# Two attention layers on one core: maxima in pairs, masks added by VectorE, and the heads of layer 0 taken in the order 0, 2, 1, 3

## What is computed

```
xn = layernorm(x)
x  = x + attention0(xn) + ffn0(xn)      # layer 0
xn = layernorm(x)
x  = x + attention1(xn) + ffn1(xn)      # layer 1
```

```
scores = einsum('bqhd,bkhd->bhqk', xq, xk) / sqrt(16)
scores = where(tril, scores, -inf)
out    = einsum('bhqk,bkhd->bqhd', softmax(scores), xv)
```

## Time and profile before

| | us |
|---|---|
| median of three runs | 1993.01 (1991.43 to 1997.32) |
| the profiled execution | 2006.2 |
| its span, first to last instruction | 2004.5 |
| TensorE busy in it | 1914.6 (96%) |
| VectorE busy | 1379.2 (69%) |
| ScalarE busy | 1088.6 (54%) |
| attention of layer 0, first score product to last | 498.66 to 1232.5 |
| attention of layer 1 | 1467.43 to 1968.8 |

### The profile page before, as it was taken

The page is one execution under the profiler, slowest core; times in us unless marked ns, Lnnn a source line. Parts: engine busy times, 40 slices in busy tenths (PEclk is TensorE's granted clock), DMA queues, the critical chain, the costliest instruction groups (busy, mean ns, idle before and its releaser), DMA issues.

```text
span 2004.5 us, 28840 instructions
## 1 busy us (share of the span) xinstructions
PE 1914.6 (96%) x10864; PEld 975.3 (49%) x10864; DVE 1379.2 (69%) x1719; ACT 1088.6 (54%) x2177; POOL 232.4 (12%) x606
## 2 busy tenths in 40 slices
PE   6999999999999999999999999999999999999998
PEld 5888887733333333333334335744543333333436
DVE  6554544425899999999996763756787777777733
ACT  4221212122787878878775774312257777677662
POOL 1000000000000000100000100000023433333330
PEclk9999999988999999999997899999999999999999
DMA  6010100043112211112212000103312212212102
GB/s 211 1 48 0 44 1 1 10 122 90 30 32 69 49 32 31 34 31 44 44 31 54 7 8 6 54 16 83 90 33 52 47 32 52 45 35 52 30 10 87
DMA packets 79211, 87.52 MB, mean 44 GB/s; under 512 B 19072, under 2 KB 52864, under 8 KB 79072
## 3 DMA queue, kind: packets, MB, share of 16 engines
q1 hardware_dynamic: 79072, 85.67, 17.2%
HBM read 55.20 MB, written 20.71 MB: 38 GB/s over the span
## 4 chain that ended last, share of the span: by engine, by line
PE 81%; ACT 7%; DVE 4%; SPq 4%; issue 2%; DMA 2%; POOL 0%; DVEq 0%; POOLq 0%; ACTq 0%; PEldq 0%
PE ps L1498 19%; PE ps L1528 11%; PE ps L1179 8%; PE ps L1180 7%; PE ps L1181 7%; PE ps L1435 7%; ACT arena L806 6%; PE ps L1524 6%; PE ps L1356 5%; PE ps L1362 4%; PE ps L1273 3%; SPq L468 2%; SPq L466 1%; DMA slots<-arena 1%; DVE arena L1043 1%
## 5 line engine op out<-in xcount | busy, mean ns | idle before, releaser
L806 ACT ACTIVATE arena<-ps 128x512 f32<-128x512 f32 (+3 forms) x1792 | 867.7, 556 | 325.5 <-PE ps L1528 171.4
L1043 DVE TENSOR_REDUCE arena<-ps 128x1 f32<-128x1024 f32 (+3 forms) x768 | 856.1, 1153 | 181.0 <-PE ps L1362 104.8
L1498 PE MATMUL ps<-arena 128*17 128x512 f32 (+3 forms) x3584 | 439.2, 562 | 1.0 <-ACT arena L806 0.6
L1362 PE MATMUL ps<-slots 48*128 48x512 f32 x1024 | 409.7, 474 | 8.8 <-DMA slots<-kparts 4.6
L1528 PE MATMUL ps<-slots 50*128 50x512 f32 x1024 | 387.9, 459 | 24.0 <-ACT arena L806 14.7
L1528 PEld LDWEIGHTS ps<-slots 50*128 50x128 f32 x1024 | 172.7, 188 | 326.7 <-ACT arena L806 269.1
L1524 PE MATMUL ps<-slots 98*128 98x512 bf16 (+3 forms) x768 | 207.7, 328 | 9.2 <-DMA slots<-arena 5.8
L1356 PE MATMUL ps<-slots 96*128 96x512 bf16 (+3 forms) x768 | 193.6, 328 | 13.8 <-DVE arena L1046 7.7
L1362 PEld LDWEIGHTS ps<-slots 48*128 48x128 f32 x1024 | 171.8, 190 | 66.7 <-DVE arena L1043 22.9
L606 POOL TENSOR_SCALAR_AFFINE_SELECT arena<-arena 128x128 f32<-128x128 f32 x512 | 145.3, 295 | 320.3 <-ACT arena L806 312.4
L667 ACT ACTIVATE xn<-ps 128x512 f32<-128x512 f32 (+1 forms) x44 | 26.3, 598 | 259.1 <-PE ps L1181 259.1
(11 more groups left out here) (127 smaller groups left out, 1855.3 us busy)
## 6 DMA issues: line engine op xcount, KB each, us to landing
slots<-qparts SPq DMA_DIRECT2D x96, 128.0 KB, 3.6
qparts<-arena SPq DMA_DIRECT2D x32, 256.0 KB
xnT<-arena SPq DMA_DIRECT2D x256, 32.0 KB
slots<-qparts SPq DMA_DIRECT2D x96, 64.0 KB, 3.3
qparts<-arena SPq DMA_DIRECT2D x48, 128.0 KB
slots<-qparts SPq DMA_DIRECT2D x32, 192.0 KB, 3.7
w_raw<-in_wgu SPq DMA_DIRECT2D x20, 256.0 KB, 3.2
acc<-in_x SPq DMA_DIRECT2D x4, 1024.0 KB, 8.0
```

Of the source, the lines that this page charges most:

```text
L806: act.activation(prob[local % P_RING][:, q0:CH], bank(local % SP_RING)[:, q0:CH], ACT.Exp, scale=SCALE).then_inc(S["p_ready"], 1)
L1043: dve.tensor_reduce(maxes[c][:, h[0] * TPC + qt:h[0] * TPC + qt + 1], src[:, 0:w], AX_X, ALU.max).then_inc(S["x_done"], 1)
L1362: last = pe.matmul(dst[:, k0:k1], q_slot[u][r:r + ROWS[0], c, h % 2, qt * P:(qt + 1) * P].bitcast(F32R), k_slot[u][r:r + ROWS[0], k0:k1].b ...
L1498: mm = pe.matmul(bank(7)[32 * h:32 * h + DH + 1, q0:CH], v_slot[n % SLOTS][:, kt, :], prob[idx % P_RING][:, q0:CH], start=(kt == 0), stop= ...
```

## The change

Five edits:

1. In layer 0 all groups take their main items in the head order 0, 2, 1, 3.
2. The first maxima of layer 0 come in pairs, behind k = 1 and k = 3, from projection 13 on, and the four pieces of a pair are sorted by key half, so that heads of both halves of the array alternate. `lower` moves behind k = 1. SyncE writes the first rows before the stores of projection 17, not 18 (`ROWS_AT`).
3. Behind the rows VectorE no longer waits for its own last operation before it raises `x_done`; TensorE waits for `m_ready` where it reuses that bank.
4. In layer 1, for the second half of queries (c = 1), the product that adds the mask is gone: VectorE adds the mask, widened to 1024 columns with zeros, and takes the maximum in one `tensor_tensor_reduce`, whose full result goes to the unused `w_q`.
5. The mask tile is widened from 128 to 1024 columns of bfloat16, which GpSimd fills at the start.

```diff
-FIRST_MAX_AT = 12
-ROWS_AT = [18, 20]
+FIRST_MAX_AT = 13
+ROWS_AT = [17, 20]
 
-    return [(kt, h, max(0, kt - TPC * qc) * P if causal else 0) for kt in range(kts) for h in range(HG)]
+    heads = range(HG) if causal else (0, 2, 1, 3)
+    return [(kt, h, max(0, kt - TPC * qc) * P if causal else 0) for kt in range(kts) for h in heads]
 
-    j = 3 * (i - FIRST_MAX_AT) + k
-    return range(j, j + 1) if i >= FIRST_MAX_AT and k < 3 and j < count else range(0)
+    j = 4 * (i - FIRST_MAX_AT) + k - 1
+    return range(j, min(j + 2, count)) if i >= FIRST_MAX_AT and k % 2 else range(0)
 
+def masked_by_vector(causal, c):
+
+    return causal and c > 0
 
-        mask_qk = sb("mask_qk", [P, P], BF16)
+        mask_qk = sb("mask_qk", [P, N], BF16)
...
-                    dve.wait_ge(S["m_ready"], n * QC + c + 1)
                     dve.sem_inc(S["x_done"], 1)
+
+                def reduce_maximum(src, n, c, qt, h, j):
+
+                    w, seg = max_width(l == 1, c, qt), segment(l == 1, c, qt)
+                    if masked_by_vector(l == 1, c):
+                        masked = w_q[:, 2 * (j % 2):2 * (j % 2) + 2, :].rearrange("p k f -> p (k f)")
+                        dve.tensor_tensor_reduce(out=masked[:, 0:w], in0=src[:, 0:w], in1=mask_qk[:, N - w:N], scale=1.0, scalar=LOWEST,
+                                                 op0=ALU.add, op1=ALU.max,
+                                                 accum_out=maxes[c][:, h[0] * TPC + qt:h[0] * TPC + qt + 1]).then_inc(S["x_done"], 1)
+                        return
...
-                            if k == 0 and i:
+                            if k == 1 and i:
                                 lower(i - 1)
...
                     if opens and j >= 2:
 
                         pe.wait_ge(S["x_done"], j if (n, c, qt) == (GROUPS - 1, 1, None) else j - 1)
+                        m, mc, mqt, _ = all_items[j - 2]
+                        if m is not None and mqt is None:
+                            pe.wait_ge(S["m_ready"], m * QC + mc + 1)
...
-                                         start=True, stop=k1 < w)
-                        if k1 == w:
-                            last = pe.matmul(dst[:, w - P:w], identb[:, :], mask_qk[:, :], start=False, stop=True)
+                                         start=True, stop=k1 < w or masked_by_vector(causal, c))
+                        if k1 == w and not masked_by_vector(causal, c):
+                            last = pe.matmul(dst[:, w - P:w], identb[:, :], mask_qk[:, N - P:N], start=False, stop=True)
...
-                    for piece in first:
-                        if piece[0] in items:
...
+                    todo = [piece for piece in first if piece[0] in items]
+                    if not causal:
+                        todo.sort(key=lambda piece: piece[5])
+                    for piece in todo:
```

More of the change, by code:

```diff
@@ L34 @@
 MASKED = -1e30
+LOWEST = -3e38
 SLOTS = 3
@@ L543, in _ @@
                                    pattern=[[-1, P]], channel_multiplier=1).then_inc(const_b, 1)
[L544 removed]
+            pool.affine_select(out=mask_qk[:, N - P:N], in_=mask_qk[:, N - P:N], compare_op=ALU.is_ge, fill=MASKED, base=0,
                                pattern=[[-1, P]], channel_multiplier=1).then_inc(const_b, 1)
@@ L771, in _ @@
                             split(NCH * NQ + t)
-                items = [main_items(l == 1, c) for c in range(QC)]
                 group_items = per_group[l]
@@ L801, in attend @@
                         for c in range(QC):
-                            for i, (kt, h, q0) in enumerate(items[c]):
+                            for i, (kt, h, q0) in enumerate(main_items(l == 1, c)):
                                 act.wait_ge(S["s_ready"], local + 1)
@@ L1286, in _ @@
                 causal = l == 1
-                items = [main_items(causal, c) for c in range(QC)]
                 group_items = per_group[l]
@@ L1336, in _ @@
                 blocks = max_blocks(l == 1)
-                items_in_all = sum(len(b) for b in blocks)
+                all_items = [item for b in blocks for item in b]
+                items_in_all = len(all_items)
                 starts = [sum(len(b) for b in blocks[:n]) for n in range(GROUPS)]
@@ L1443, in first_maxima @@
                 def first_maxima(items):
-                    for piece in first:
-                        if piece[0] in items:
-                            if piece[0] == 0 and piece[-2]:
-                                pe.wait_ge(S["slot_in"][0], 16 * 12)
-                                pe.wait_ge(*((S["b_evac"], TT) if l else (S["y_evac"], TT * len(ROUNDS) + 1)))
-                            max_piece(*piece)
+                    todo = [piece for piece in first if piece[0] in items]
+                    if not causal:
+                        todo.sort(key=lambda piece: piece[5])
+                    for piece in todo:
+                        if piece[0] == 0 and piece[-2]:
+                            pe.wait_ge(S["slot_in"][0], 16 * 12)
+                            pe.wait_ge(*((S["b_evac"], TT) if l else (S["y_evac"], TT * len(ROUNDS) + 1)))
+                        max_piece(*piece)
                 if l == 0:
@@ L1515, in attend @@
                         for c in range(QC):
-                            nkt = len(items[c]) // HG
-                            for i, (kt, h, q0) in enumerate(items[c]):
+                            items = main_items(causal, c)
+                            nkt = len(items) // HG
+                            for i, (kt, h, q0) in enumerate(items):
                                 if i == 0:
```

29 lines of the change are left out of this document (15 added, 14 removed).

## The result

The changed kernel takes 1969.4 us in the median of 15 runs (1964.66 to 1992.46); the kernel before, run beside it, takes 1996.8 (1983.86 to 2008.41, also 15). The ratio is 0.9886, 95% interval 0.9851 to 0.9921: faster by 1.1%. An execution over 1.5% above the fastest of its kernel counts as slow and is left out of every median and ratio here (none of these two kernels, two of `e4_heads_only`, three of `e6_singles13`, of which one took 4555.6 us). The profiled execution takes 1973.01 us against 2006.2, and its span is 33.2 us shorter.

A forecast was written before the change was run, and what follows sets the result against it. Layer 0's attention was taken as bound by the ring of three banks through ScalarE. Terms -17.2 - 12.6 - 3.0 = -32.8 us took 2006.2 to 1973.4, less 13.2 for the median: 1960 us, range 1938 to 1993.

The forecast's parts named there:

- the likeliest case: Whole kernel: the forecast of 1960 us holds, own range 1948 to 1970; chance 0.58.
- the last step: Whole kernel: from 1973.4 us for the profiled execution, 13.2 taken off for the median, giving 1960.
- First maxima (-17.2): Layer 0's first maxima: standstill and half clock go, pairs 3.21 us apart, first score product at 481.4 instead of 498.66.
- Masks (-12.6): Layer 1's second parts: 15 x 14 mask products of 0.06 us go, VectorE stays hidden; -12.6 us.
- Pauses (-3.0): VectorE behind the rows, both layers: 60 pauses shrink by some 0.1 us, half of 6 us taken; -3.0 us.
- Head order (0): Layer 0's quads: a fifth step lies in the wait for ScalarE, the quad stays 2.60 us; 0 us.
- the small slip: Rival, layer 0: the fifth step lengthens quads by 0.02 to 0.1 us, time 1965 to 1984; chance 0.09.
- The wide mask (0): Kernel start: filling the wide mask costs GpSimd under a microsecond more, ahead of any product; nothing.
- The clock didn't fall in the first maxima: Rival, layer 0's first maxima: the clock falls all the same, 17.6 us of gain lost, time 1977; chance 0.12.
- The weight load isn't paid: Rival, layer 0's quads: same-half products pay weight loads, 0.2 to 0.36 us a quad, time 2008 to 2046; chance 0.11.
- VectorE isn't the bound in layer 1: Rival, layer 1's second parts: half-speed fused operation makes VectorE the bound, 158 us, time 2130; chance 0.04.
- Group 13 kept its clock: Rival, layer 0's group 13: some 20 us of its 72.2 come back, time 1940; chance 0.06.

The follow-up runs named there:

- e4_heads_only: The kernel before with only the head order 0, 2, 1, 3 in layer 0: 1994.6 us, ratio 1.0013 to before.
- e6_singles13: The kernel before with first maxima from projection 13, one item behind each step, not paired; first rows from item 17: 1992.0 us, ratio 0.9983 to before.
- e5: The kernel before with only VectorE's pause behind the rows removed (TensorE waits for `m_ready` instead): 1993.2 us, ratio 0.9978 to before.
- e1: The changed kernel with head order 0, 1, 2, 3 restored in layer 0, all other edits kept: 1962.4 us, ratio 0.9848 to before.
- e7: The kernel before with paired first maxima but still from projection 12, first rows from item 16: 1988.0 us, ratio 0.9967 to before.
- e9: The changed kernel with head order 0, 1, 2, 3 in layer 0 and layer 1's second-part rows written ahead of stores: 1960.0 us, ratio 0.9818 to before.
- e10: The changed kernel with head order 0, 1, 2, 3 in layer 0, run once more in more rounds: 1964.1 us, ratio 0.9842 to before.
- e3: The kernel before with only the mask edits (mask added in VectorE, widened mask tile): 1982.5 us, ratio 0.9942 to before.
- e2: The kernel before with only the pairs of first maxima, from projection 13: 1979.3 us, ratio 0.9937 to before.
- e8: The kernel before with layer 0's maxima in head order 0, 2, 1, 3 instead of 2, 0, 3, 1: 2046.9 us, ratio 1.0238 to before.

## Why the prediction was right, and where it was off

**The time.** 1960 was forecast, 1969.4 measured, inside the range of 1938 to 1993 and at the edge of the likeliest case's own (1948 to 1970). The forecast for the profiled execution, 1973.4, met its 1973.01, but only since errors cancelled there; that is luck. The 9.4 us by which the median was missed all lie in the last step, where I took off 13.2 us because the profiled execution before stood that far above its median: the one after stood only 3.6 above. Against the sum of -32.8, the first maxima gave 3.0 more and group 13 gave 17.2 that were not in it; the masks and pauses together gave 10.3 instead of 15.6 (5.3 less), the head order cost 5.2, group 11 and the last group 5.3 (each holds a fall of the clock of 6.8 us that the trace before doesn't have there), a fall in layer 1 (one group of 32.99 us) and small things there 3.3, the ends 0.7. That is -20.2 and +19.8. The median gained 27.4, not 33.2: the trace before was of an execution 9.4 us above the median of its 15 runs, that of after 3.6 above; 33.2 - 9.4 + 3.6 = 27.4. I read the length of falls in one trace as part of the kernel: "what followed the standstill" was a fall of 24 us in that trace and in e5, and of 6.8 to 13.7 in four others, and group 13 "at clock 0.69" took 55 us at full clock in seven of the ten traces of other kernels whose quads are as long (after, e1 to e7, e9, e10). The floor that I gave for group 13 at full clock, 47 us, was too low.

**First maxima (-17.2).** Mechanism right: the standstill gone, and with it the half clock; e7 and the count over all traces show the one with the other. The pace was mis-sized: 2.95 us a pair for 3.21. I said that a pair opens "only when both reductions of the pair before are done". Its first piece needs the bank of the first of these reductions alone, and starts while the second runs (444.96). When that ends (445.37), the opening piece of the pair's other item and the closing piece of the first item start together on the two halves (445.42), and the reduction 0.54 later: 0.60 us between reductions, not 0.85. With 2.95 us a pair the last one opens at 471.4, not 474.4, and that is the 3.0. Of a fall of 13.7 us, as e3 and e4 show it, the gain is 14.9, of which 4.8 is the later start (e7 against e2) and the rest the pairs and the length of the fall, which no run separates; not all of it shows in the timed runs, where the pairs alone gave 0.6% in the ratio (some 12 us), and 10.1 us in the column "at 0.990", which leaves the clock's share out.

**Masks (-12.6).** Mechanism right, 0.06 us each where TensorE is the bound (0.11 to 0.12 a quad with two). The first two quads of the second part wait for VectorE or a DMA and give 0.04 and 0.03 instead of 0.12 each; a group gives 0.66 to 0.69, not 0.84, in all 10 us. VectorE stays hidden. The reading of the accumulator was taken as 0.10 us on top of a reduction; fused operation and reading together are 0.01 to 0.02 longer than a plain reduction, although the record of the reading says 0.08. The Trainium skill (VectorE: DVE Perf Modes, Two Vector instructions with no wait between them) has such an operation as two instructions: the trace shows both, and their price is nearly that of one.

**Pauses (-3.0).** Nothing; the price was the wrong step. The pause did go (in layer 1 the next operation starts 0.21 us behind the start of the last row operation, 1602.73 to 1602.94 in the trace after, where the earlier trace rows have 0.43; in layer 0 of e5 it is 0.34), but VectorE had idle time in the next quad to catch up, and what it hands over earlier lies ahead of the wait of the fourth score product. I had taken half without a reason; "at least none where VectorE catches up anyway" was the case.

**Head order (0).** Right for the plain quad in what counts: the fourth score product at 1.18, the closing piece 0.24 later, the quad 2.60. Wrong in the quad behind the rows, +0.20 twice a group. "With no room left" was the warning, and I went on to sum only plain quads. In the rows quad two delays add up: VectorE's reductions already end 0.2 later, so the opening piece does too (0.84 for 0.63), and the closing piece comes another 0.24 behind it, since a score product of its half now stands between. VectorE, done with the rows, has to wait for it and begins its reductions 0.37 later than in the old order, with the pause (e4) as without it; that delay reaches the opening piece of the next quad (1.16 for 0.80) and with it the step behind the wait, where nothing hides it. It is 0.4 us a group, 0.025 a quad on average: the small slip among the rivals, 0.02 to 0.1, which had a chance of 0.09 and whose 1965 to 1984 holds the measured time.

**The wide mask (0).** Right: the mask is ready at 3.3 us instead of 2.6, long ahead of TensorE's first instruction at 11.4 (11.7 before).

**The rivals.** The clock didn't fall in the first maxima. The weight load isn't paid: plain quads are as long as before. The rule of the Trainium skill (TensorE: Matmul & The Clock Gate, Part 3), by which a load overlaps matmuls in flight only on another row group, does not hold here; the same part elsewhere also allows a load into a background weight buffer, and with that the traces agree: in e8 loads start beside a product of their own half, and products follow each other there at 0.24 us. VectorE isn't the bound in layer 1. Group 13 kept its clock in the trace after, the rival with a chance of 0.06; but e1 and e10 are one kernel and took 55.4 and 65.7 us there (in e10 and e9 the clock fell for 27 us), so this is no effect of the change.

Still open: what makes the clock fall in group 13 in one execution and not in the next; no run here varied that alone. The sorting of the pieces by key half wasn't tried apart from the pairs either. The size of each part in the timed runs rests on the common slope of 15 us per 0.01; the ratios alone leave the order of the change and `e1_order0123` likely but not certain.

## What to carry to other kernels

Where an engine waits in the middle of a repeated pattern, as TensorE does here for ScalarE, steps ahead of that wait can be free while steps behind it are not: ask of each moved instruction on which side of the wait it falls, and ask it again for the odd iterations (here the one that makes the rows), whose slack is smaller. Before a stage of one trace enters a sum, look whether its clock is full and whether its like in other executions has the same length: 17 of the 33 us between these two traces were a chance. And a small DMA that stands behind stores in a queue is worth moving before anything is shaved from the engines: it gave some 7 us for three lines.

## What the runs showed of the hardware

- A fused add and maximum of VectorE (PSUM and bfloat16 in, float32 out, with accumulator) of 1024 columns is spaced 1.15 us, its reading of the accumulator included; a plain maximum 1.13 to 1.14.
- At a standstill of TensorE of 4.06 to 4.89 us the granted clock fell to half (1.2 GHz) in six traces of six, for 6.8, 10.2, 13.7 or 24 us, although the engine was busy again; with a wait of 0.20 to 1.20 us at the same place it stayed full in seven of seven.
- In dense group 13 it fell in some executions, for 27 us in e10, with TensorE busy 26.4 us of them:

```profile
1053.50:1080.80 27.30, 26.41 (x109) 0.50 0.24 44
```

- Successive products on one half of the array follow each other at 0.23 to 0.24 us (0.33 to 0.34 behind the first one after a wait) for 512 columns of float32 on 50 or 48 partitions, with their weight loads hidden.
